# Two stages of a graph and mixture-of-experts kernel in one block, with the first loads issued by ScalarE

## The reference

```python
def _L0_gnn_ref(x, W, edge_row, edge_col, edge_val):
    h = jnp.einsum('nd,od->no', x, W)
    return jax.ops.segment_sum(edge_val[:, None] * h[edge_col], edge_row, num_segments=6250)

def _L0_ffn_ref(x, gate_w, gate_b, w1, b1, w2, b2, gamma, beta):
    topk_vals, topk_idx = jax.lax.top_k(x @ gate_w + gate_b, 2)          # 16 experts
    topk_w = jax.nn.softmax(topk_vals, axis=-1)
    h = jax.nn.relu(jnp.einsum('bsh,ehf->bsef', x, w1) + b1)
    expert_out = jnp.einsum('bsef,efh->bseh', h, w2) + b2
    sel = jnp.take_along_axis(expert_out, topk_idx[:, :, :, None], axis=2)
    y = x + jnp.sum(topk_w[..., None] * sel, axis=2)
    return (y - mean(y)) / jnp.sqrt(var(y) + EPS) * gamma + beta
...
x = x + _L0_gnn_ref(_layernorm(x, axis=-1), L0_gnn_W, src, dst, edge_weight)
x = x + _L0_ffn_ref(_layernorm(x, axis=-1)[None], ...)[0]
```

## Time and profile before

| | us |
|---|---|
| median of 3 runs | 2129.42 |
| lowest and highest | 2127.3, 2132.4 |
| the profiled execution | 2131.93 |
| its span, from the first to the last instruction | 2129.9 |
| experts' stage in the trace, first request to last real tile's sum | 1565.5 to 2002.2 |
| last stage in the trace, first load to the end | 2015.03 to 2129.9 |

### The profile page before, as it was taken

The page is one execution under the profiler, slowest core; times in us unless marked ns, Lnnn a source line. Parts: engine busy times, 40 slices in busy tenths (PEclk is TensorE's granted clock), DMA queues, the critical chain, the costliest instruction groups (busy, mean ns, idle before and its releaser), DMA issues. The chain is left out here.

```text
span 2129.9 us, 33319 instructions
## 1 busy us (share of the span) xinstructions
PE 1480.1 (69%) x7822; PEld 1164.8 (55%) x7823; DVE 978.4 (46%) x2239; ACT 507.8 (24%) x1490; POOL 1276.2 (60%) x1156
## 2 busy tenths in 40 slices
PE   6007888057767677777777777776169999989563
PEld 4007887034545454554454545554159989978552
DVE  8999999033333332323333333233743333323265
ACT  4542111000101010101010101010635444434363
POOL 1003999757777777777777777777025545544423
PEclk9559999557887887878788888788589999999886
DMA  5111000023333333333333333334542232263363
GB/s 169 35 35 54 3 2 2 14 86 105 104 104 103 103 104 104 104 105 103 104 103 104 103 104 103 103 103 101 137 153 71 70 106 70 89 190 111 102 209 111
DMA packets 107264, 201.62 MB, mean 95 GB/s; under 512 B 19940, under 2 KB 68699, under 8 KB 107096
## 3 DMA queue, kind: packets, MB, share of 16 engines
q0 software_dynamic: 52672, 139.93, 22.6%
q1 hardware_dynamic: 43352, 46.50, 6.7%
q10 hardware_dynamic: 11200, 14.68, 2.2%
HBM read 165.17 MB, written 35.86 MB: 94 GB/s over the span
## 5 line engine op out<-in xcount | busy, mean ns | idle before, releaser
L805 POOL DMA_INDIRECT hbuf<-xn_rows,ix x832 | 798.3, 960 | 273.0 <-issue 237.4
L848 PE MATMUL bank<-hbuf,picks 128*128 x2032 | 661.0, 466 | 275.0 <-SPq L793 274.2
L848 PEld LDWEIGHTS bank<-hbuf,picks 128*128 128x128 f32 x2032 | 418.2, 225 | 498.1 <-issue 443.5
L831 DVE TENSOR_SCALAR picks<-iota_two,marks 128x256 f32<-128x256 f32 x832 | 332.5, 442 | 701.7 <-PE bank L848 686.3
L376 POOL DMA_INDIRECT edge_groups<-work,dest_i x56 | 215.7, 3853 | 201.2 <-DVE work L584 184.7
L719 PE MATMUL bank<-work 128*128 128x192 bf16 x1568 | 146.7, 251 | 130.3 <-DVE work L577 130.3
L1312 PEld LDWEIGHTS bank<-rowsT,w_sb 128*128 128x128 f32 x1744 | 212.3, 193 | 28.9 <-issue 24.2
L1312 PE MATMUL bank<-rowsT,w_sb 128*128 128x128 f32 x1744 | 215.6, 277 | 17.9 <-issue 17.9
L914 ACT ACTIVATE agg<-bank 128x256 f32<-128x256 f32 x49 | 18.8, 383 | 870.8 <-PE bank L848 870.8
L1254 POOL DMA_INDIRECT expert_out<-y_sb,to_i x112 | 111.1, 992 | 168.9 <-DVE y_sb L1356 159.0
L719 PEld LDWEIGHTS bank<-work 128*128 128x128 bf16 x1568 | 135.1, 98 | 135.3 <-issue 134.7
(11 more groups left out here) (247 smaller groups left out, 1323.3 us busy)
## 6 DMA issues: line engine op xcount, KB each, us to landing
w_sb<-in_L_ffn_w_dram ACTq DMA_DIRECT2D x28, 512.0 KB, 5.0
hbuf<-xn_rows,ix POOLq DMA_INDIRECT x832, 2.8
xn_rows<-xn SPq DMA_DIRECT2D x11, 896.0 KB, 4.0
ya<-expert_out SPq DMA_DIRECT2D x7, 896.0 KB, 5.9
yb<-expert_out SPq DMA_DIRECT2D x7, 896.0 KB, 7.9
x<-in_x_dram SPq DMA_DIRECT2D x6, 896.0 KB, 11.1
out_dram<-o SPq DMA_DIRECT2D x7, 512.0 KB, 2.9
xn_rows<-x SPq DMA_DIRECT2D x3, 896.0 KB, 4.0
```

The source lines that it names most:

```text
L805: pool.indirect_dma_start(hbuf[:, 1 + j, k, :], None, xn_dram, bass.IndirectOffsetOnAxis(ap=ix[:, 2 * j + k:2 * j + k + 1], axis=0)).then_ ...
L831: s = v.tensor_scalar(picks[:, j % 2, k, :], iota_two[:], marks[:, 0, 2 * j + k:2 * j + k + 1], marks[:, 1, 2 * j + k:2 * j + k + 1], ALU. ...
L848: m = nc.tensor.matmul(bk[q][:, 0:D], picks[:, j, k, q * P:(q + 1) * P], hbuf[:, ds(place + j, 1), k, :].rearrange("p s d -> p (s d)"), st ...
```

## The change

Three edits, to the last two stages only:

1. The experts' block and the last block are one `nc.Block`. The last stage's code becomes functions (`last_sync`, `last_tensor`, `last_scalar`, `last_gpsimd`, `last_vector`) that each engine calls behind its part of the experts' stage. The barrier between is gone, and the buffers of both stages stand in memory side by side.
2. The loads of groups 0 and 1 are started by ACT instead of SP: behind `share(0)`, and behind waits that count the sends of the real tiles in each of the four send semaphores. The other five groups stay with SP.
3. In POOL's loop step s sends tile s first and then requests tile s + 4.

```diff
             @block.gpsimd
                 with pool.Fori(0, fours) as i:
                     for k in range(AH):
+                        pool.wait_ge(y_ready, i * AH + (k + 2))
+                        pool.sem_inc(pool_steps, 1)
+                        pool.indirect_dma_start(y_dram, ..., y_sb[:, k % 2, :], None).then_inc(y_sent[k], 16)
                         pool.wait_ge(numbers_set, i * AH + (AH + k + 1))
                         pool.wait_ge(rows_set, i * AH + (k + 1))
                         pool.sem_inc(pool_steps, 1)
                         gather(k)
-                        pool.wait_ge(y_ready, i * AH + (k + 2))
-                        pool.sem_inc(pool_steps, 1)
-                        pool.indirect_dma_start(y_dram, ..., y_sb[:, k % 2, :], None).then_inc(y_sent[k], 16)
+                last_gpsimd(pool)
...
                 act.sem_inc(rows_set, AH - 2)
+                last_scalar(act, tiles)
...
-        expert_stage.close()
-        with nc.Block() as block:
-            @block.sync
-            def _(sp):
-                load(0)
-                load(1)
...
+        def last_scalar(act, tiles):
             share(0)
+            for k in range(AH):
+                act.wait_ge(y_sent[k], ((tiles + (AH - 1 - k)) >> 2) * 16)
+            load(act, 0)
+            load(act, 1)
             for t in range(WT):
```

More of the change, by code:

```diff
@@ L1218, in nothing @@
             pass
+        ya = [sb(f"ya{q}", [P, WB, D], fp32) for q in range(2)]
+        yb = [sb(f"yb{q}", [P, WB, D], fp32) for q in range(2)]
+        o = [sb(f"o{q}", [P, WB, D], fp32) for q in range(2)]
+        shares = sb("shares", [P, WB, 2, P], fp32)
+        stats3 = sb("stats3", [P, WB, 6], fp32)
+        mv3 = sb("mv3", [P, WB, 2], fp32)
+        std3 = sb("std3", [P, WB], fp32)
+        rs3 = sb("rs3", [P, WB], fp32)
+        sh3 = sb("sh3", [P, WB], fp32)
+        HALVES = [(0, WB // 2 + 1), (WB // 2 + 1, WB // 2)]
@@ new lines, in gnn_moe_kernel @@
+        LATE = 2
+        ya_in = [sem(f"ya_in{q}") for q in range(2)]
+        yb_in = [sem(f"yb_in{q}") for q in range(2)]
+        shares_ready = sem("shares_ready")
+        y_summed = sem("y_summed")
+        o_added = sem("o_added")
+        mv3_ready = sem("mv3_ready")
+        std3_ready = sem("std3_ready")
+        norm3_ready = sem("norm3_ready")
+        yn_ready = sem("yn_ready")
+        last_ready = sem("last_ready")
+        scaled = sem("scaled")
+        late_scaled = sem("late_scaled")
@@ new lines, in last_tensor @@
+        def last_tensor(pe):
+            for t in range(WT):
+                q = t % 2
+                pe.wait_ge(ya_in[q], 16 * (t // 2 + 1))
+                pe.wait_ge(yb_in[q], 16 * (t // 2 + 1))
+                for j in range(WB):
+                    w = t * WB + j
+                    pe.wait_ge(shares_ready, w + 1)
+                    if w >= 8:
+                        pe.wait_ge(o_added, w - 7)
+                    nc.tensor.matmul(summed(w), shares[:, j, 0, :], ya[q][:, j, :], start=True, stop=False)
+                    nc.tensor.matmul(summed(w), shares[:, j, 1, :], yb[q][:, j, :], start=False, stop=True).then_inc(y_summed, 1)
@@ L1235, in _ @@
                         sp.sem_inc(y_gone, 1)
+                last_sync(sp)
             @block.gpsimd
@@ L1324, in _ @@
                 experts(pe, start, tile, nothing)
+                last_tensor(pe)
             @block.vector
@@ L1523, in gnn_moe_kernel @@
-        last_stage.close()
+                last_vector(dve)
 _INS = ['x', 'src', 'dst', 'edge_weight', 'L0_gnn_W', 'L0_ffn_gate_w', 'L0_ffn_gate_b', 'L0_ffn_w1', 'L0_ffn_b1',
```

204 lines of the change are left out of this document (91 added, 113 removed).

## The result

The changed kernel takes 2120.1 us (median of 6 runs, 2119.66 to 2122.01) beside 2128.9 us for the kernel before in the same comparison: ratio 0.9959, 95% interval 0.9946 to 0.9972. It is faster by 8.8 us, where 6.3 us had been forecast. The profiled execution took 2121.47 us (span 2119.7) instead of 2131.93 (span 2129.9).

The account below looks back on a forecast made before the run. PE bounds the experts' stage; at the seam it idles 21.9 us while loads wait for pads and barrier. Gain 6.5 - 0.2 = 6.3 us, so 2129.42 - 6.3 = 2123.1 us; range 2119.5 to 2127.5.

Parts of the forecast that it names:

- Shares done: At the seam, ACT leaves its loop in 1.5 us and ends the 14 shares near 2005.5, hidden behind the last send.
- Last real send and its landing: At the seam, the last real tile's send stays at 2003.55 and lands 2.8 us later, at 2006.35, setting the loads.
- Issue of `yb`: At the seam, ACT issues the `yb` load near 2006.9, after 0.1 us for the wait and 0.43 us to issue.
- Flight: First `yb` load: 7.58 us as before plus 2.0 us for pads beside it, bounds 0 and 2.5 us.
- PE's start: Last stage: PE starts at 2016.6 instead of 2023.13, a gain of 6.5 us, bounds 6.0 and 8.6.
- every us at PE's start moves the end by the same us: Last stage: its ring waits for nothing outside, so PE's first matmul moving ahead moves the end equally.
- the same slow start, moved along: Last stage: PE's clock again returns to full some six us behind PE's start; full clock from the start bounds 3 us.
- that rival's number: Last stage, PE's clock does not fall or returns sooner: gain 9 us, time 2120; chance 8%.
- Edit 3: POOL's loop in the experts' stage: sending before requesting loses 0.2 us, with 1.77 us of cover per tile.
- The second rival: Experts' stage: requests land too late beside weight loads, ACT copies late, PE waits; costs 10 us, time 2133; chance 7%.
- the pads hold the loads: At the seam, pads delay `yb` to 11 to 14 us behind issue; gain 2 to 5 us, 2127; chance 15%.
- the loads still wait: At the seam, loads start 2 to 5 us later through a pad's send or late ACT; 2127; chance 5%.

Follow-up runs that it names:

- e7: Changed kernel, but DVE lets POOL send the pads only when group 0's loads have landed; 2474.4 us, ratio 0.9982 to the kernel before.
- e11: Changed kernel with SP reporting the send first, pads held until group 0's loads land, and those loads split in two; 2496.7 us, ratio 0.9986 to kernel before.
- e1_again: Changed kernel without any edit, run again in a later series; 2476.3 us, ratio 0.9987 to the kernel before.
- e8: Changed kernel with 30 unused matmuls on PE while it waits for the last stage's loads; 2475.2 us, ratio 0.9984 to the kernel before.
- e6: Changed kernel, but each request on POOL also waits for the next tile's y_sb sum; 2567.4 us, no ratio given.
- e2: Changed kernel with POOL's request ahead of the send again, as in the kernel before; 2474.4 us, ratio 0.9980 to the kernel before.
- e9: Changed kernel, but SP reports the send of tile s before the rows of tile s + 4; 2500.1 us, ratio 0.9995 to the kernel before.
- e5_before: The kernel before without any edit, run in a later series for its trace; 2476.4 us.

## Why the prediction was right, and where its terms were off

The direction and the mechanism held, 2120.1 lies in the range, and it is 3.0 us under the forecast. Of these, 1.75 us are the tail, 0.5 us the seam, 0.2 us the stage and 0.5 us the median of the kernel before, which came out at 2128.9 instead of 2129.42. Step by step, with the times of after moved by the 1.4 us that its start was earlier:

- *Shares done*: forecast 2005.5, measured 2004.8. ACT needed 0.82 us between experts and shares, not 1.5.
- *Last real send and its landing*: forecast 2003.55 + 2.8, measured 2003.0 + 2.43. I had left the send where it was, since "a request stands ahead of it too". In fact the long step moved from the send to that request: 2.22 us idle there, then the send at once.
- *Issue of `yb`*: forecast 2006.9, measured 2006.2.
- *Flight*: forecast 7.58 + 2.0, measured 9.80; e7 shows the same load at 7.57 us without the pads. This was the least certain term, and 2.2 lies between its two bounds. The Trainium skill, "DMA: Bandwidth & Descriptors", section "Queues, rings and completion order", says that a DMA engine takes turns between its queue rows packet by packet. From that I had worked out that the loads pay 2.5 us and the pads hardly anything. The loads' part agrees about as well as mine; the pads' doesn't, since they land after 7.0 us.
- *PE's start*: forecast 2016.6, measured 2016.1. The gain at the seam is 7.0 us for 6.5. That every us at PE's start moves the end by the same us held for this change, but not in general: in e11 the seam is 4.4 us shorter than in e1_again and the tail 1.6 us longer, since SP's load of group 2 comes late.
- *Clock*: "the same slow start, moved along" was the step that failed. The clock was back 3.2 us behind PE's start, not 6, and the tail is 1.75 us shorter. I had this as a rival (3 us, 8%, with a return within three us as its sign) and not as a part of the sum. That 2120.1 is also that rival's number is luck: e1_again had the same short pause, a return after 5.9 us and no shorter tail. Over the kernels of the table, e8 apart, the return lies between 2.9 and 6.1 us behind PE's start. The two tails of the first series, 105.0 and 106.7 us, go with that. In the later ones the link is loose: e6 has 2.9 us and 105.3, e2 5.3 and 105.6, e7 6.1 and 105.7. The tail of the kernel before alone differs by 1.1 us between two traces (106.7 and 105.7), so how much of the 1.75 us is the clock stays open; by the store above it is 1.0 us at the most.
- *Edit 3*: forecast 0.2 us lost, measured 0.0 in 424.3. The sums were right for this series, but they bounded the wrong thing. The second rival placed a loss at the ends of experts beside the weight loads, and said that late requests would be its cause. In the later series the loss is there, 3 to 6 us, at that place; but ACT's copies are not late, PE's own groups are. So the place was right, the mechanism was not, and the price of 10 us was about twice too high.

Of the rivals, "the pads hold the loads" is out (9.80 us, not 11 to 14; 11.1 only in e2, where the first pad starts ahead of the load), and "the loads still wait" is out by the chain. One bound of the forecast does not follow from its terms: 6.0 us at the seam less 0.8 in the stage is a gain of 5.2 and not 4.5 us. Nothing hung on it.

## What to carry to other kernels

Ask of each load behind a phase what its wait really needs: here the gain came from waiting for the real tiles' sends alone, while the barrier itself was worth 1.1 us, by one pair of traces. A serial relay of semaphores is a hidden order: before moving an issue, check what is reported behind it. In e6, where the requests come late, it cost 0.67 us a tile over the stage; in the changed kernel, where they don't, exchanging the reports gave nothing (e9). And a reordering that costs nothing in one series (0.0 us) can cost 3 to 6 us in others; measure it again, on another chip too, before keeping it for a gain of 3 us.

## What I had not expected of the hardware

- POOL has a step 1.9 to 2.6 us longer than the others at the 114th and 220th indirect DMA of the stage (idle for 4.05 us ahead of a send where 1.47 is usual, 2.22 us ahead of a request where 0.30 is). It stands at the same place in the count in all kernels here, whichever of send and request that is. Its cause is open.
- The same kernel takes 2129 us in one series, 2479 us on chip 7, and 2478 and then 2502 us on chip 6. So the chip's number alone does not explain the differences. The experts' stage differs by only 2 us (424.3 and 426.2); most lies ahead of it, since the first `y_sb` stands at 1577.5 in the first series and at 1921.4 in e5_before.
- Two queues that share the DMA engines both pay: a load's first flight 9.8 instead of 7.6 us, the pads' sends 7.0 instead of 2.8.
- The granted clock fell for 3.41 us in the middle of the experts' stage (0.60 in a window of 3 us), with PE busy for 3.90 of 5 us shortly before it and never idle for more than 2.00 us at a time.
